# The node stage of a two-layer graph network, moved into the edge loop of layer 0

## The reference

```python
# layer 0
h = x @ Wx.T + bx
A = W_ac - W_ac.T - 0.1 * eye(128)
q, k, v = h @ Wq.T + bq, h @ Wk.T + bk, h @ Wv.T + bv
e = concat([msg, cos(abs(last_update[src] - t) * time_w + time_b)]) @ We.T
alpha = softmax over the edges of one dst of (q[dst] * (k[src] + e)).sum(-1) / sqrt(128)
m = segment_sum((v[src] + e) * alpha, dst)
x = layernorm(x + tanh(h + tanh(h @ A.T + m + b_ac)))
# layer 1
edge_new = relu(concat([x[src], x[dst]]) @ We1 + be1) @ We2 + be2
agg = segment_sum(edge_new, dst)
x = layernorm(x + x + relu(concat([x, agg]) @ Wn1 + bn1) @ Wn2 + bn2)
```

## Time and profile before

| | us |
|---|---|
| three runs, median (lowest to highest) | 5235.6 (5226.69 to 5240.83) |
| profiled execution, first to last instruction (span) | 4156.7 |
| median less span | 1078.9 |
| layer 0 loop, first to last gather issue | 53.3 to 2012.1 |
| node stage block, from its first DMA issue to the first instruction of layer 1 | 2053.55 to 2172.30 |
| layer 1 loop, from its first gather | 2175.20 |
| busy share of the span: PE, DVE, ACT, POOL | 75%, 59%, 42%, 73% |

### The profile page before, as it was taken

One profiled execution on the slowest core, in us unless ns is written; L12 is line 12 of the kernel. 1 busy time (PEld: TensorE's weight loads), 2 busy tenths in 40 slices (PEclk: granted clock), 3 DMA queues, 4 the chain that ended last, 5 costly groups with the idle time before them and its releaser, 6 DMA issues. The chain is left out here.

```text
span 4156.7 us, 73778 instructions
## 1 busy us (share of the span) xinstructions
PE 3100.8 (75%) x18778; PEld 2820.4 (68%) x18779; DVE 2472.7 (59%) x5456; ACT 1733.9 (42%) x2900; POOL 3014.0 (73%) x3193
## 2 busy tenths in 40 slices
PE   6888887888888888888666666666667677766675
PEld 4777777777777777777546666666666666666665
DVE  4877777777777777777574444444444444454544
ACT  3767776777777777777461111111111111111111
POOL 5777777777777777777347777777777777777775
PEclk8999999999999999999896666666666666767677
DMA  6333333333333333333233333333333333333332
GB/s 187 81 81 83 81 83 81 83 81 82 82 81 82 81 82 82 81 82 82 75 102 101 89 92 89 92 89 91 91 89 93 91 96 93 94 95 94 94 95 61
DMA packets 419860, 370.13 MB, mean 89 GB/s; under 512 B 269651, under 2 KB 347883, under 8 KB 419724
## 3 DMA queue, kind: packets, MB, share of 16 engines
q0 software_dynamic: 100032, 217.87, 20.5%
q1 hardware_dynamic: 308544, 143.31, 13.5%
q10 hardware_dynamic: 11214, 8.17, 0.7%
HBM read 347.56 MB, written 21.44 MB: 89 GB/s over the span
## 5 line engine op out<-in xcount | busy, mean ns | idle before, releaser
L721 POOL DMA_INDIRECT he<-h_table,src_i x1563 | 1477.5, 945 | 515.7 <-issue 505.3
L1642 POOL DMA_INDIRECT msg<-p_table,src x1563 | 1474.8, 944 | 484.1 <-issue 484.1
L1659 PE MATMUL p_edge<-r_win,hotT 80*128 80x128 f32 x3136 | 656.7, 395 | 589.2 <-DVE msg L1780 575.2
L1659 PEld LDWEIGHTS p_edge<-r_win,hotT 80*128 80x128 f32 x3136 | 606.6, 297 | 630.5 <-issue 536.8
L1715 ACT ACTIVATE msg<-msg 128x1024 f32<-128x1024 f32 x196 | 207.2, 1057 | 1649.0 <-DVE msg L1780 1649.0
L1780 DVE TENSOR_TENSOR msg<-msg,p_edge 128x512 f32<-128x512 f32 x392 | 251.9, 684 | 979.1 <-DMA msg<-p_table,src 979.1
L1670 PE MATMUL p_sumT<-msg,hot 128*80 128x129 f32 x3136 | 601.0, 372 | 34.4 <-ACT sumT L1723 34.4
L1670 PEld LDWEIGHTS p_sumT<-msg,hot 128*80 128x80 f32 x3136 | 580.0, 224 | 51.3 <-issue 51.2
L760 PE MATMUL p_score<-qk_two,heT 128*128 128x160 f32 x1568 | 394.9, 335 | 166.2 <-ACT heT L870 164.4
L762 PE MATMUL p_score<-qk_win,heT 128*128 128x80 f32 x3136 | 462.7, 272 | 0.0
L762 PEld LDWEIGHTS p_score<-qk_win,heT 128*128 128x128 f32 x3136 | 451.9, 199 | 0.0
(11 more groups left out here) (205 smaller groups left out, 4114.8 us busy)
## 6 DMA issues: line engine op xcount, KB each, us to landing
dst_row<-in_dst_dram SPq DMA_DIRECT2D x196, 320.0 KB
feat<-in_edge_attr_dram SPq DMA_DIRECT2D x196, 128.0 KB
he<-h_table,src_i POOLq DMA_INDIRECT x1563
msg<-p_table,src POOLq DMA_INDIRECT x1563
qk_win<-qk_table SPq DMA_DIRECT2D x196, 40.0 KB
qk_two<-qk_table SPq DMA_DIRECT2D x392, 20.0 KB
r_win<-r_table SPq DMA_DIRECT2D x196, 40.0 KB
qk_table<-qk SPq DMA_DIRECT2D x13, 512.0 KB
```

The costliest lines, as they stand in the source:

```text
L721: e.indirect_dma_start(out=he[u][:, j, 2 * FE:2 * FE + ROW], out_offset=None, in_=h_table[:, :], in_offset=bass.IndirectOffsetOnAxis(ap=sr ...
L1642: e.indirect_dma_start(out=msg[u][:, j, 0:D], out_offset=None, in_=p_table[:, :], in_offset=bass.IndirectOffsetOnAxis(ap=src_i[u][:, j:j + ...
L1659: mm = e.matmul(p_edge[h][:, j % 4, :], hotT_of(c)[:, j, :], r_win[u][:, :], start=True, stop=True)
```

## The change

The node stage as a block is gone. Its work is done inside layer 0's chunk loop, in turns 15 to 27, one group of four blocks per turn (13 groups, k = 0 to 12), at the block `block_i[k]` below which `acc` is final; two more groups (numbers 13 and 14) follow at the end of layer 0, one after the other. Groups can overlap, so that 15 groups cover 49 blocks.

- The stage works with nodes on partitions: we_bvT gets a 129th column that picks out the denominator, so that each block's product has it as its column 129; the trip of the denominators through DRAM is gone.
- Both tables come from one product of 256 columns per block (`node_tables`), one addition writes both (`node_copy_rows`).
- `hT` is stored to DRAM (`hT_dram`, 3.4 MB) by one DMA in front of the loop; SBUF of hT is then used for the stage's buffers. h, x and hT of a group are loaded back per turn (`node_load`, on SP's queue, 256 KB each); x1T, p and r are stored from ACT's queue (`node_store`, `node_store_rows`).
- PE waits at three places before its `turn`: for `pre_done` at u = 1, `x1T_done` at u = 5, `rows_done` at u = 6, since the stage uses the PSUM banks `p_turn` in between.
- Layer 1 clears `acc` itself, on DVE, loads its weights itself, loads x1T per group (`load_x1`), and adds 2 x1 by four more products with 2 I per group (`mesh`).

```diff
+            def node_take(e, n, b, k):                      # ACT, behind step u = 0
+                e.wait_ge(x1_full, val(e, n + 1))
+                e.activation(node_acc, acc[:, 0, bass.ds(at, G)], ACT.Copy)
+                e.activation(node_m[k][0:A2, :, :], by_block(acc[0:A2, 1, bass.ds(at, G)]), ACT.Copy).then_inc(acc_taken, 1)
+            def node_values(e, n, k):                       # PE, inside step u = 1
+                e.wait_ge(rows_done, val(e, n + 1))
+                for j in range(GB):
+                    e.matmul(bank[:, at:at + D + 1], second[:, j, :], we_bvT[:, :], start=True, stop=False)
+                    e.matmul(bank[:, at:at + D], first[:, here], wvT[:, :], start=False, stop=True)
+                    mm = e.matmul(p_turn[0][:, here], node_hT[:, here], aT[:, :], start=True, stop=True)
+                mm.then_inc(val_full, 1)
+            def node_pre(e, n, k):                          # DVE, behind step u = 1
+                e.wait_ge(val_full, n1)
+                for q in range(2):
+                    op = e.tensor_scalar(node_den[k][:, 2 * q:2 * q + 2], dens, 1.0e-16, None, ALU.add)
+                e.tensor_tensor(node_m[k], by_block(p_turn[0][:, :]), bac_b..., ALU.add).then_inc(anti_done, 1)
+                e.reciprocal(node_rden[k], node_den[k]).then_inc(rden_done, 1)
+                for j in range(GB):
+                    op = e.scalar_tensor_tensor(out=node_m[k][:, j, :], in0=p_turn[1 + j // 2][:, at:at + D], ...)
+                op.then_inc(pre_done, 1)
...
+            def node_copy_rows(e, n):                       # DVE, behind step u = 6
+                e.wait_ge(tables_full, val(e, n + 1))
+                for q in range(2):
+                    op = e.tensor_tensor(both_rows[:, 2 * q:2 * q + 2, :], p_turn[q][:, :]..., be1_b..., ALU.add)
+                op.then_inc(rows_done, 1)
...
-                        chunks(e, load, apart_first=load_apart)
+                            e.dma_start(hT_dram[:, :], hT[:, :]).then_inc(hT_out, 16)
+                            chunks(e, load, apart_first=load_apart, grouped=load_grouped, ahead=1)
...
+                        def step_grouped(c, k):             # PE
+                            if u == 1:
+                                step(c, lambda: node_values(e, k, 0), lambda: e.wait_ge(pre_done, val(e, k + 1)))
+                            elif u == 5:
+                                step(c, lambda: node_turn(e, k, 0), lambda: e.wait_ge(x1T_done, val(e, k + 1)))
+                            elif u == 6:
+                                step(c, lambda: node_tables(e, k), lambda: e.wait_ge(rows_done, val(e, k + 2)))
...
+                            e.wait_ge(pre_done, GROUPS)     # PE, the end of layer 0
+                            node_turn(e, GROUPS - 1, 1)
+                            node_tables(e, GROUPS - 1)
+                            node_values(e, GROUPS, None)
+                            node_turn(e, GROUPS, 0)
+                            node_tables(e, GROUPS)
...
+                            if u == 2:                      # ACT
+                                step(c, lambda: node_update(e, k, 0))
+                            elif u == 3:
+                                step(c, lambda: node_tanh(e, k, 0))
+                            elif u == 4:
+                                step(c, lambda: node_root(e, k, 0))
+                            elif u == 5:
+                                step(c, lambda: node_copy_x1(e, k))
...
+                            step(c)                         # DVE
+                            if u == 1:
+                                node_pre(e, k, 0)
+                            elif u == 2:
+                                node_h2(e, k, 0)
+                            elif u == 3:
+                                node_moments(e, k, 0, 0)
+                            elif u == 4:
+                                node_normal(e, k, 0)
+                            elif u == 6:
+                                node_copy_rows(e, k)
...
+                            e.memset(acc[:, 0, :], 0.0)     # layer 1, DVE
+                            e.memset(acc[0:1, 1, :], 0.0)
```

More of the change, by code:

```diff
@@ new lines, in node_update, with node_h2, node_tanh @@
+            def node_update(e, n, k):
+                e.wait_ge(pre_done, val(e, n + 1))
+                e.sem_inc(passed, 1)
+                e.activation(node_m[k], node_m[k], ACT.Tanh).then_inc(upd_done, 1)
+            def node_h2(e, n, k):
+                e.wait_ge(upd_done, val(e, n + 1))
+                e.wait_ge(node_h_in, val(e, n * 16 + 16))
+                e.tensor_tensor(node_m[k], node_m[k], node_h[k], ALU.add).then_inc(h2_done, 1)
+            def node_tanh(e, n, k):
+                e.wait_ge(h2_done, val(e, n + 1))
+                e.sem_inc(passed, 1)
+                e.activation(node_m[k], node_m[k], ACT.Tanh).then_inc(tanh_done, 1)
@@ new lines, in node_moments @@
+            def node_moments(e, n, k, rest):
+                n1 = val(e, n + 1)
+                e.wait_ge(tanh_done, n1)
+                e.wait_ge(node_x_in, val(e, n * 16 + 16))
+                if rest:
+                    e.wait_ge(node_rest_in, 16 * rest)
+                e.tensor_tensor(node_m[k], node_m[k], node_x[k], ALU.add).then_inc(y_done, 1)
+                e.wait_ge(y_done, n1)
+                e.sem_inc(passed, 1)
+                for j in range(GB):
+                    op = e.bn_stats(node_stats[k][:, j, :], node_m[k][:, j, :])
+                op.then_inc(stats_done, 1)
+                e.wait_ge(stats_done, n1)
+                e.sem_inc(passed, 1)
+                for j in range(GB):
+                    op = e.bn_aggr(node_mv[k][:, j, :], node_stats[k][:, j, :])
+                op.then_inc(mv_done, 1)
@@ new lines, in node_root, with node_normal @@
+            def node_root(e, n, k):
+                e.wait_ge(mv_done, val(e, n + 1))
+                e.sem_inc(passed, 1)
+                e.activation(node_std[k], node_mv[k][:, :, 1:2].rearrange("p b o -> p (b o)"), ACT.Sqrt, bias=eps_c[:, 0:1]).then_inc(root_done, 1)
+            def node_normal(e, n, k):
+                n1 = val(e, n + 1)
+                e.wait_ge(root_done, n1)
+                e.reciprocal(node_rstd[k], node_std[k]).then_inc(rstd_done, 1)
+                e.wait_ge(rstd_done, n1)
+                e.sem_inc(passed, 1)
+                for j in range(GB):
+                    op = e.tensor_scalar(node_m[k][:, j, :], node_m[k][:, j, :], node_mv[k][:, j, 0:1], node_rstd[k][:, j:j + 1], ALU.subtract, ALU.mult)
+                op.then_inc(xn_done, 1)
@@ new lines, in node_turn, with node_copy_x1 @@
+            def node_turn(e, n, k):
+                e.wait_ge(xn_done, val(e, n + 1))
+                for j in range(GB):
+                    mm = e.transpose(p_turn[1][:, j * P:(j + 1) * P], node_m[k][:, j, :], ident[:, :])
+                mm.then_inc(x1_full, 1)
+            def node_copy_x1(e, n):
+                e.wait_ge(x1_full, val(e, n + 2))
+                e.sem_inc(passed, 1)
+                e.wait_ge(x1T_out, val(e, n * 16 + 1))
+                e.sem_inc(passed, 1)
+                e.activation(x1T_g, p_turn[1][:, :], ACT.Copy).then_inc(x1T_done, 1)
@@ L695, in _ @@
                                 load_src((0, u))
+                            chunks(e, load, apart_first=load_apart)
                         else:
@@ L825, in _ @@
                         turn((0, 1))
-                        chunks(e, step)
+                        if at_first:
+                            e.sem_inc(x1_full, 1)
+                            chunks(e, step, grouped=step_grouped, ahead=1)
+                        else:
+                            chunks(e, step)
                         spread_top((TURNS - 1, SLOTS - 1))
@@ L1085, in _ @@
                         masks((0, 0))
-                        chunks(e, step)
+                        if at_first:
+                            e.sem_inc(rows_done, 1)
+                            e.sem_inc(p_out, 1)
+                            e.sem_inc(r_out, 1)
+                            chunks(e, step, grouped=step_grouped, ahead=1)
+                        else:
+                            chunks(e, step)
                         add((TURNS - 1, SLOTS - 4), starts[3])
@@ L1127, in gnn_kernel @@
         layer0.close()
-        x1_rows = sb("x1_rows", [P, BLOCKS, D])
-        x1T = hT
+        x1_g = [sb(f"x1_g{k}", [P, G]) for k in range(2)]
         bn2_b = sb("bn2_b", [P, D])
@@ L1477, in gnn_kernel @@
             fixed = sem("fixed1")
+            loads = sem("loads1")
+            x1_in = sem("x1_in")
+            w_full = sem("w_full1")
+            w_done = sem("w_done1")
+            LOADS1 = 16 * 6
             out_done = sem("out_done1")
@@ L1825, in _ @@
                         if at_first:
[L1826 removed]
+                            moments(e, GROUPS)
                             normal(e, GROUPS)
```

572 lines of the change are left out of this document (297 added, 275 removed).

## The result

The changed kernel took 5291.0 us (median of 4, 5283.1 to 5305.4), the kernel before beside it 5234.3: a ratio of 1.0116, 95% interval 1.0096 to 1.0136. Forecast were 5177 us and a faster kernel.

What follows compares the result with a forecast made beforehand. The prediction took POOL's gathers to pace layer 0, with the node stage unoverlapped on the path. It summed -118.75 + 9 + 49.6 + 2 = -58.1 us: span 4098.6, time 5177 us, range 5155 to 5235.

Steps and rivals of the forecast that it cites:

- in 70.0 us there are 12.6 us of room: Layer 0 loop: POOL paces a 70.0 us turn; without POOL it would take 57.4, leaving 12.6 us.
- the 1078.9 us around the span I carry over unchanged: Whole kernel: span 4156.7 us against a run median of 5235.6; the difference was assumed to stay.
- the loop forecast at 0: Layer 0 loop: node work moved into the turns was to add 0 us, as it fits beside POOL's pace.
- The extras per turn (10.3): Layer 0 loop: 7.7 us of DVE node work plus 2.6 us of bubbles per turn, against 12.6 of room.
- I allow 0.5 and 1.0 us of DVE bubble: Layer 0 loop: allowance for PE's `turn` standing behind DVE's step at u = 1 and u = 6.
- The start: +9: Loop's start: the hT store delays the index loads for POOL's eighth chunk; +9 us, bounds 0 to 15.
- The end: -80 net: Last addition of layer 0 to layer 1: 44.9 us forecast, -80.0 net of the removed node stage.
- The doubled PE work at 1.2 GHz: End of layer 0: PE, mostly idle, runs at 1.2 instead of 2.4 GHz, adding 6.75 us.
- Layer 1: +2: Layer 1: clearing acc and loads are hidden; eight more product records in `mesh` at the end cost +2 us.
- The loop becomes bound by DVE and PE: Rival, layer 0 loop: extras exceed the 12.6 us room, PE's waits may cost its clock; 5249 us, chance 0.18.
- POOL's issues are slowed: Rival, layer 0 loop: POOL stands still during DVE's `normal` instructions, 21 us, time 5198; chance 0.07.
- The stage isn't hidden: Rival: node stage serial at the end, for instance SP's late loads hold up the windows; 78 us, 5255; chance 0.02.

Runs made afterwards that it cites:

- pe_wide: Kernel before, first product of each pair in layer 0's scores issued three times instead of once: 4172.8 us beside 4166.8, ratio 1.0015.
- no_loads: Changed kernel without a group's three loads in the grouped turns: 4117.8 us beside 4166.8 (0.9879); 1.0121 beside 5194.5.
- pe_quarter: Changed kernel, PE's node work in grouped turns cut to one block of four: 4105.7 us beside 4166.8 (0.9854); 1.0108 beside 5194.5.
- after_3: Profiled run of the changed kernel, nothing edited, in the session where before took 5194.5 us: ratio 1.0113.
- waits: Kernel before plus one PE wait for DVE's reduction (top_j) at u = 1 and u = 6, no added work: 5252.1 us beside 5173.1, 1.016.
- early: Changed kernel, PE's node work ahead of its step's scores and all DVE node work ahead of the masks: 5148.1 us beside 5173.1, 0.9955.

## Why the prediction was wrong

**The step that failed is "in 70.0 us there are 12.6 us of room"**, together with "the 1078.9 us around the span I carry over unchanged". 1078.9 us that no instruction accounts for should have been the warning: this trace can't be of an execution like those timed. In the timed ones the span is 2 us short of the time, the turn has 91.5 us instead of 70.0, and POOL isn't the pacemaker but waits about 3 us in each chunk. At the level of the trace the room is there (pe_wide), or nearly (no_loads 1.3 us over 70.0 a turn, pe_quarter 0.6). The whole error of 114 us is this term: the loop forecast at 0 cost some 120.

**The extras per turn (10.3) against the loss (9.8)** look like a hit and are none. They were to be DVE's 7.7 and bubbles of 2.6; moving DVE's 4.3 changed nothing, and a quarter of PE's work cost as much as all of it. "I allow 0.5 and 1.0 us of DVE bubble" for PE's waits at u = 1 and u = 6 was the right place with the wrong consequence: what counts is not DVE's bubble but the bursts of POOL that start late, by 2.7, 2.2 and 4.7 us a turn at u = 6, 0 and 1. The sum had no term for the largest of the three, PE's products ahead of the sums at u = 1.

**The start: +9.** Measured +6.6: the 57th gather starts at 175.24 instead of 168.67 us in the two traces of one session:

```profile
168.67 0.94 POOL L721 DMA_INDIRECT he<-h_table,src_i  x1 [47.97 <-PE p_sum L786]
```

```profile
175.24 0.94 POOL L963 DMA_INDIRECT he<-h_table,src_i  x1 [53.34 <-DMA src_i<-in_src_dram]
```

POOL waits 48 us for the first sums even without the store. In the changed kernel's first profile SP issues the store, then the indices, and then POOL goes on:

```profile
161.66 0.36 SPq L945 DMA_DIRECT2D hT_dram<-hT  x1
162.51 3.02 SPq L888 DMA_DIRECT2D src_i<-in_src_dram  x3
```

```profile
174.12 0.95 POOL L963 DMA_INDIRECT he<-h_table,src_i  x1 [53.69 <-DMA src_i<-in_src_dram]
```

12.5 us from the store's issue, with the indices as what ended the wait, as the 11.4 us at 299 GB/s had it. At the level of the forecast's trace the term was too large: the wait is 9.8 us in no_loads and 10.3 in pe_quarter, not 14, and the gather starts 0.7 and 2.0 us later than at 128.49, since SP issued the store at 115.7 and 117.3, not at 121; in pe_quarter even the sums ended the wait, not the indices. The ring order that the Trainium skill states ("DMA: Bandwidth & Descriptors", Queues, rings and completion order) agrees with this.

**The end: -80 net.** Forecast 44.9 us from the last addition to layer 1, measured 43.75. The doubled PE work at 1.2 GHz was right to charge: the chain of groups 13 and 14 takes 34.6 us of the 35.6 charged with it, against 28.9 without, at a granted clock of 0.66. The end is the same at both levels, 43.8 us in no_loads too. (Group 14's terms add up to 18.75, not 18.85, and the bubbles of the loop to 2.5, not 2.6; neither matters.)

**Layer 1: +2.** Measured +0.4, its clearing of `acc` (twice 5.6 us) hidden as said. Layer 1 differs by more than that between sessions, so the term isn't tested.

**The rivals.** "The loop becomes bound by DVE and PE" had the sign and the place, PE's new waits, with 0.18, but its limit was the same 12.6 us. Its price, PE's clock in `sums`, is there at two of the three late steps: in after_3 the granted clock during the sums is 0.68 at u = 0 and 0.66 at u = 1, and they take 5.8 and 4.2 us; in the kernel before it is 0.88 and 0.93, and they take 3.3 and 3.0. In waits the clock is 0.94 at the late steps, so a wait costs without it. How much of the changed kernel's loss is clock wasn't tested, and early, whose clock there is 0.90 and 0.81, doesn't tell the two apart. "POOL's issues are slowed" didn't happen, 947 against 944 ns. "The stage isn't hidden" named SP's loads, which cost nothing (no_loads). No rival had the case that the trace shows another pace than the timed runs, which deserved a chance of its own and a range up to the forecast without any room: 10.3 x 13 = 134 us more, 5311. That would have held 5291.

## What to carry to other kernels

Before a trace is used, hold its span against the times: if hundreds of us lie outside it, the trace is of another pace, and room read from it (who waits for whom, and how long) doesn't carry over, while the chain of work at the end, which nothing competed with, did (43.8 us at both levels). A wait put on an engine in a pipelined loop is paid by what that engine releases later in its order. It can cost much without guarding any work, 79 us here, and one test tells: add the wait alone. Where borrowed buffers force a wait, try the borrowing ahead of the loop's own work, so that the wait is over when the engine comes to it; here that got back half of the loss. And look at what stands ahead of the instruction that others wait for: the products put there at u = 1 came with the other half.

## What the runs showed of the hardware

- The same program takes 4167 or about 5200 us (medians of 5168 to 5234), steady within a session but for the two executions named with the result. At the slower level nearly every chunk of layer 0 has a stretch of some 4 us in which instructions of SP take about 0.7 us each and PE's come 0.7 to 1.4 us apart. In the chunk shown DVE, ACT and POOL go on within 1 us of each other, up to 7 us after PE had done what they wait for.
- What causes it is open. The kernel before's slower trace holds 24,190 records of semaphore changes, the quick one 96,587, at equal numbers of instructions; all 15 slower traces hold 23,500 to 25,200, all five quick ones 94,300 to 97,000. The Trainium skill, "NOTIFIC — the notification-queue block", section Overflow: three behaviours, one of which stalls the engine, says that a full record queue can drop records or hold up the engine that writes them. That would fit both marks, but no run here takes the recording away, so it is a guess.
- Within that level the loop takes some additional work almost free: 1.24 us on DVE per chunk cost 0.16 to 0.19, four memsets on POOL behind the gathers nothing (between them 15 us in all). It charges for what puts the end of the sums later than about 13 us behind the burst: waits of PE, or PE's work ahead of the sums.
